# A two-layer graph network on one core: the first layer sorted in three parts of 72, 128 and 200 columns, GpSimd left with gathers alone, the norm split on ScalarE and VectorE, the relation weights made on TensorE

## The reference

```python
h = relu(layernorm(x))
neigh = segment_sum(h[src], dst, num_segments=3125)
x = x + relu(relu(((1 + eps) * h + neigh) @ W1 + b1) @ W2 + b2)

h = relu(layernorm(x))
weights = einsum('rb,bio->rio', coefficients, bases)      # 16 relations from 8 bases
msg[e] = h[dst[e]] @ weights[type[e]]
x = x + (h @ w_self.T).at[src].add(msg)
```

## Time and profile before

| | |
|---|---|
| three runs | 1696.48 us median (1687.71 to 1698.53) |
| profiled execution: span, first to last instruction | 1680.4 us |
| the profiled execution's own time | not listed apart from the three runs, which lie 7.3 to 18.1 us above its span |
| TensorE matmuls busy | 933.3 us, 56%, 5317 instructions |
| TensorE weight loads busy (they overlap) | 656.0 us, 39%, 5318 |
| VectorE busy | 749.9 us, 45%, 2213 |
| ScalarE busy | 413.4 us, 25%, 977 |
| GpSimd busy | 911.3 us, 54%, 843 |
| transfers | 101.58 MB, 60 GB/s; 43955 of 73343 packets under 512 bytes |

### The profile page before, as it was taken

The page is one execution under the profiler, slowest core; times in us unless marked ns, Lnnn a source line. Parts: engine busy times, 40 slices in busy tenths (PEclk is TensorE's granted clock), DMA queues, the critical chain, the costliest instruction groups (busy, mean ns, idle before and its releaser), DMA issues.

```text
span 1680.4 us, 22781 instructions
## 1 busy us (share of the span) xinstructions
PE 933.3 (56%) x5317; PEld 656.0 (39%) x5318; DVE 749.9 (45%) x2213; ACT 413.4 (25%) x977; POOL 911.3 (54%) x843
## 2 busy tenths in 40 slices
PE   1355275666238676766678997145354345453535
PEld 0223153444114344443356444134353344343535
DVE  8888463665934444593457543012121122121213
ACT  4662263552014333443345431000000000000000
POOL 4354655555866566765560003746656656566562
PEclk9955586777657777876789998567676567665667
DMA  3010222224122222212221685211111111111113
GB/s 73 0 57 20 73 52 61 54 55 57 47 67 60 54 56 59 59 41 60 57 57 10 196 285 152 54 35 43 44 40 45 45 36 47 40 43 44 39 46 55
DMA packets 73343, 101.58 MB, mean 60 GB/s; under 512 B 43955, under 2 KB 52836, under 8 KB 73036
## 3 DMA queue, kind: packets, MB, share of 16 engines
q0 software_dynamic: 33120, 67.88, 16.3%
q1 hardware_dynamic: 40166, 33.09, 7.2%
HBM read 70.88 MB, written 29.60 MB: 60 GB/s over the span
## 4 chain that ended last, share of the span: by engine, by line
PE 44%; issue 28%; DVE 12%; another core or an unknown queue 12%; ACT 1%; DVEq 1%; DMA 1%; POOL 1%; ACTq 0%; SPq 0%; POOLq 0%
PE ps L802 16%; PE ps L819 15%; PE ps L824 9%; PE ps L893 4%; DVE spare L554 1%; DVE chunk_hot L616 1%; ACT place_val_b L443 1%; DVE spare L587 1%; DVE node_hot L668 1%; DVE chunk_f L590 1%; DVE place_val_a L619 1%; DVE w_rel L679 1%; DVE spare L678 1%; POOL gathered L411 1%
## 5 line engine op out<-in xcount | busy, mean ns | idle before, releaser
L411 POOL DMA_INDIRECT gathered<-h_table,row_stage x420 | 469.9, 1119 | 309.8 <-issue 247.4
L411 POOL DMA_INDIRECT gathered<-z_table,row_stage x405 | 385.5, 952 | 385.8 <-issue 229.0
L819 PE MATMUL ps<-gathered,node_hot 128*125 128x128 f32 x1620 | 289.6, 326 | 350.1 <-issue 328.5
L443 ACT ACTIVATE place_val_b<-place_hot,code_b 125x128 f16<-125x128 f16 x800 | 343.8, 522 | 523.1 <-DVE place_hot L612 361.2
L819 PEld LDWEIGHTS ps<-gathered,node_hot 128*125 128x125 f32 x1620 | 258.4, 235 | 381.4 <-issue 381.1
L668 DVE TENSOR_SCALAR node_hot<-iota_f,key_of 128x250 f32<-128x250 f32 x405 | 130.6, 364 | 512.5 <-remote 368.6
L802 PE MATMUL ps<-chunk_hot,place_val_a 125*128 125x405 f16 (+2 forms) x800 | 280.0, 364 | 117.1 <-DVE place_val_a L619 58.6
L802 PE MATMUL ps<-chunk_hot,place_val_b 125*128 125x387 f16 (+3 forms) x1200 | 274.5, 292 | 50.0 <-issue 41.2
L824 PE MATMUL ps<-node_hot,gathered 128*128 128x250 bf16 x1260 | 193.6, 299 | 156.8 <-issue 117.6
L616 DVE TENSOR_SCALAR chunk_hot<-iota_h,chunk_f 125x405 f16<-125x405 f16 (+2 forms) x800 | 210.2, 341 | 13.1 <-issue 12.6
L824 PEld LDWEIGHTS ps<-node_hot,gathered 128*128 128x128 bf16 x1260 | 127.6, 106 | 211.1 <-issue 188.0
(11 more groups left out here) (128 smaller groups left out, 319.1 us busy)
## 6 DMA issues: line engine op xcount, KB each, us to landing
z_table<-spare SPq DMA_DIRECT2D x50, 448.0 KB
gathered<-h_table,row_stage POOLq DMA_INDIRECT x420
gathered<-z_table,row_stage POOLq DMA_INDIRECT x405
z_table<-spare SPq DMA_DIRECT2D x50, 52.0 KB
h_table<-gathered SPq DMA_DIRECT2D x1, 2100.0 KB
x_sb<-in_x SPq DMA_DIRECT2D x1, 1400.0 KB
out<-x_sb SPq DMA_DIRECT2D x6, 224.0 KB
row_stage<-row_of SPq DMA_DIRECT2D x81, 2.5 KB
```

The source lines that it names most:

```text
L411: pool.indirect_dma_start(place.rearrange("p j d -> p (j d)") if s < 2 else place, None, table, bass.IndirectOffsetOnAxis(ap=row_stage[s][ ...
L443: nc.scalar.activation(place_val_b[:, buf, i, :], place_hot[:, buf, :, i], ACT.Copy, scale=code_b[l][:, bass.ds(batch * BATCH + (c0 + i), ...
L819: last = T.matmul(psf[0:NP, bass.ds(offs[i] + half * D, D)], node_hot_of[s][:, k % HOTS[s], half * NP:(half + 1) * NP], gathered_of[s][:, ...
```

## The change

Layer one is sorted in three parts of 72, 128 and 200 columns, so there are four sorts. The first two use buckets of four tiles (7 buckets): their zero-one matrices and matmuls have 506 columns. The parts have 78, 132, 208 and 405 chunks, the rings hold 39, 44, 52 and 45. `BESIDE_ROUNDS` is now the whole number of rounds of the part ahead in each case but the last layer's own. The first sort has batches of its own (`sort_first`) without ScalarE: the code is multiplied into the chunk comparison. A code is now one number split in two halves, and each column takes two matmuls in every part.

GpSimd issues gathers and nothing else, written out one by one, straight from `row_of`; SyncE stages nothing. The norm's scaling and the first two parts of h are ScalarE's, the differences VectorE's, in two halves of 13 and 12 tiles. The relation weights are four matmuls of a block matrix of coefficients with the bases at the start, copied out by ScalarE, and turned to their layout through a table in memory. Layer two's sort is now decoded before the sums of layer one are copied out.

```diff
-SORTS = [(0, 0, 144, 3, 13), (0, 144, 256, 4, 11), (1, 0, 400, 5, 9)]
+SORTS = [(0, 0, 72, 4, 3, 13), (0, 72, 128, 4, 4, 11), (0, 200, 200, 2, 4, 13), (1, 0, 400, 2, 5, 9)]
+BUCKETS = [-(-TILES // tiles) for tiles in QUAD]
+WIDE = [2 * NP if tiles == 2 else 2 * NP + 2 * 128 for tiles in QUAD]
-HOTS = [13, 22, 9]
+HOTS = [13, 11, 26, 9]
-BESIDE_ROUNDS = [0, 3, 6]
-ALONE_ROUND = [0, 0, 3]
+BESIDE_ROUNDS = [0, 2, 3, 4]
+ALONE_ROUND = [0, 0, 0, 2]
...
         @block.sync
-            for p0, p1 in PARTS:
-                sp.dma_start(x_sb[p0:p1, :, :], x_rows[p0:p1, :, :]).then_inc(ld_x, 16)
+            for b in range(N_BASES):
+                sp.dma_start(bases_sb[b * IL:(b + 1) * IL, :, :],
+                             bases[b].rearrange("(ih il) o -> il ih o", il=IL)).then_inc(ld_b, 16)
-            stage_rows(sp, 0)
-            stage_rows(sp, 1)
+            for k, (t0_, t1_) in enumerate(HALVES):
+                sp.wait_ge(low_ready, k + 1)
+                for p0, p1 in PARTS:
+                    sp.dma_start(h_rows[p0:p1, t0_:t1_, :, :], h_parts[p0:p1, t0_:t1_, :, :]).then_inc(h_stored, 16)
+            sp.wait_ge(w_read, 4)
+            for m in range(2):
+                sp.dma_start(w_table.rearrange("(ih m il) (r o) -> m (il r) ih o", ih=IH, m=2, o=D)[m],
+                             w_turned[:, m * IH * D:(m + 1) * IH * D].rearrange("p (ih o) -> p ih o", o=D)).then_inc(w_stored, 16)
+            sp.wait_ge(w_stored, 32)
+            sp.dma_start(w_rel[:, :, :].rearrange("p r o -> p (r o)"), w_table).then_inc(wrel_ready, 16)
-            stage_rows(sp, 2)
...
         @block.gpsimd
-            pool.wait_ge(ld_c, 32)
-            add_bases(0, 3)
-            pool.tensor_tensor(h_sb[:, :, :], x_sb[:, :, :], neg_mean[:, :, :].to_broadcast([NP, TILES, D]),
-                               ALU.add).then_inc(centred, 1)
...
-            add_bases(3, BASES_FIRST)
-                with nc.gpsimd.Fori(0, ROUNDS[s]) as r:
-                    for g in range(GROUPS[s]):
-                        pool.wait_ge(staged[s][g], r * 16 + 16)
...
+            pool.wait_ge(h_stored, 64)
+            for s in range(NSORT):
+                pool.wait_ge(decoded, s + 1)
+                for k in range(CHUNKS[s]):
+                    slot = k % RING[s]
+                    if k % GROUP[s] == 0:
+                        if k >= RING[s]:
+                            pool.wait_ge(nhot_used, RING[0] + CHUNKS_BEFORE[s] + k + GROUP[s] - RING[s])
+                        elif s and k < RING[s - 1]:
+                            pool.wait_ge(nhot_used, RING[0] + CHUNKS_BEFORE[s] - RING[s - 1] + min(k + GROUP[s], RING[s - 1]))
+                    place = gathered_of[s][:, slot]
+                    pool.indirect_dma_start(
+                        place if s == LAST else place.rearrange("p j d -> p (j d)"), None, z_table if s == LAST else h_table,
+                        bass.IndirectOffsetOnAxis(ap=row_of[s][:, k:k + 1], axis=0)).then_inc(got[s][slot // GROUP[s]], 16)
...
         @block.scalar
+            for k, (t0_, t1_) in enumerate(HALVES):
+                for p0, p1 in PARTS:
+                    nc.scalar.dma_start(x_sb[p0:p1, t0_:t1_, :], x_rows[p0:p1, t0_:t1_, :]).then_inc(ld_x[k], 16)
+            normalise(0)
+            high(0)
+            normalise(1)
+            middle(0)
+            high(1)
+            middle(1)
+            act.wait_ge(w_ps, 4)
+            for q in range(4):
+                nc.scalar.copy(w_turned[:, q * BANK:(q + 1) * BANK], ps[:, q, :]).then_inc(w_read, 1)
...
         @block.vector
+            def sort_first(batch):
+                dve.wait_ge(batch_used, batch + 1)
+                V.tensor_tensor(place_hot[:, buf, :, :], iota_run[0:EP, :, :], each(place_h[0], P), ALU.is_equal)
+                own(V.tensor_tensor(first_hot[:, 2, buf], iota_run[0:EP, 0:FIRST, :], each(chunk_h0, FIRST), ALU.is_equal))
+                V.tensor_tensor(first_hot[:, 0, buf], first_hot[:, 2, buf], each(code_a[0], FIRST), ALU.mult)
+                V.tensor_tensor(first_hot[:, 1, buf], first_hot[:, 2, buf], each(first_b, FIRST), ALU.mult).then_inc(batch_ready, 1)
...
-            for s in (1, 2):
+            for s in range(1, NSORT):
                 rank_place(s)
...
-                rounds_beside(nc.vector, s - 1, node_hots, sort_batch, add_bases if s == 2 else None)
-                if s < 2:
-                    read_sorted(s)
-                    decode_rows(s)
-                    decode_keys(s)
-                    rounds_rest(nc.vector, s - 1, node_hots)
-                    rank_count(s + 1)
+                rounds_beside(nc.vector, s - 1, node_hots, sort_batch)
+                read_sorted(s)
+                decode(s)
+                rounds_rest(nc.vector, s - 1, node_hots)
+                if s < LAST:
+                    rank_count(s + 1)
```

More of the change, by code:

```diff
@@ new lines, in rank_count @@
+                own(V.tensor_scalar(need_i, tot_ps[:, 0:nb], float(P - 1), None, ALU.add))
+                own(V.tensor_scalar(need_i, need_i, 7, None, ALU.logical_shift_right))
+                own(V.tensor_copy(need_f, need_i))
+                own(V.tensor_tensor_scan(upto, need_f, need_f, 0.0, ALU.add, ALU.bypass))
+                nq = -(-CHUNKS[s] // P)
+                for q in range(nq):
+                    own(V.tensor_scalar(le_scr, upto, pidx[:, q:q + 1], 0.0, ALU.is_le, ALU.add,
+                                        accum_out=bucket_of[:, q:q + 1]))
@@ L781, in rank_sums @@
             def rank_sums(l):
+                nb = BUCKETS[l]
                 pe.wait_ge(count_ready, l + 1)
-                T.matmul(pre_ps, before[0:EP, 0:EP], count[:, :], start=True, stop=True)
-                T.matmul(tot_ps, ones[0:EP, :], count[:, :], start=True, stop=True).then_inc(prefix_done, 1)
+                T.matmul(pre_ps[:, 0:nb], before[0:EP, 0:EP], count_all[:, 0:nb], start=True, stop=True)
+                T.matmul(tot_ps[:, 0:nb], ones[0:EP, :], count_all[:, 0:nb], start=True, stop=True).then_inc(prefix_done, 1)
                 pe.wait_ge(bucket_of_ready, l + 1)
@@ L816, in add_up @@
                     pe.wait_ge(nhot_ready, r * RING[s] + (CHUNKS_BEFORE[s] + k + 1))
-                    for half in range(2 if s == 2 else 0):
+                    for half in range(2 if s == LAST else 0):
                         last = T.matmul(psf[0:NP, bass.ds(offs[i] + half * D, D)],
@@ L821, in add_up @@
                                         start=False, stop=False, skip_group_check=True)
-                    for part in range(SPLITS if s < 2 else 0):
-                        last = T.matmul(psf[:, bass.ds(offs[i], WIDE)], gathered_of[s][:, k, part, :],
+                    for part in range(SPLITS if s < LAST else 0):
+                        last = T.matmul(psf[:, bass.ds(offs[i], WIDE[s])], gathered_of[s][:, k, part, :],
                                         node_hot_of[s][:, k % HOTS[s], :], start=False, stop=False, skip_group_check=True)
@@ L828, in _ @@
             rank_sums(0)
-            for b in range(8):
+            zero_bank(7)
+            for b in range(2):
+                sort_first(b)
+            pe.wait_ge(kron_ready, 1)
+            pe.wait_ge(ld_b, 16 * N_BASES)
+            for m in range(2):
+                for q in range(2):
+                    T.matmul(ps[:, 2 * m + q, :], kron[:, m * IH:(m + 1) * IH, :].rearrange("p l r -> p (l r)"),
+                             bases_sb[:, q * BT:(q + 1) * BT, :].rearrange("p h o -> p (h o)"), start=True, stop=True).then_inc(w_ps, 1)
+            for b in range(2, COLS[0] // BATCH):
+                sort_first(b)
+            pe.wait_ge(w_read, 4)
+            for b in range(7):
                 zero_bank(b)
-            batches_alone(nc.tensor, 0, sort_batch, 0, ALONE[0])
-            pe.wait_ge(decoded, 1)
-            pe.wait_ge(h_ready, 1)
+            pe.wait_ge(h0_ready, 2)
             pe.wait_ge(eps_ready, 1)
```

404 lines of the change are left out of this document (192 added, 212 removed).

## The result

The changed kernel takes 1556.38 us (median of 4 runs, 1552.01 to 1560.11) against 1694.97 for the kernel before in the same comparison (4 runs, 1687.71 to 1698.53): ratio **0.918**, 95% interval 0.916 to 0.921. Predicted were 1567 us and a range of 1495 to 1660. Its profiled run took 1555.58 us, 2.0 above its span of 1553.6. The time lies in the range, 11 us under the forecast.

The account below looks back on a forecast made before the run. GpSimd's gathers, 1.25 us each plus stalls, were taken to pace both layers. 59 + 730 + 35 + 113.6 + 590.7 + 23 = 1551.3 us of span, with 16.1 above it 1567 us; range 1495 to 1660.

Parts of the forecast that it names:

- the round trip: In each gather gap, 2.4 us go over SyncE; with GpSimd waiting for TensorE itself, a gap loses 1.9 us.
- Layer two: Its gather stage: 19 gaps shortened from 6.35 us by 1.9 each, 590.7 us for 627.3, -37.
- rival 1: Gaps are not the round trip's to shorten; an earlier GpSimd only ends TensorE's free run earlier: 84 us back, 1651 (22%).
- Start: Before the first gather: smaller first sort and less GpSimd work bring it to 59 us from 144.8, -86, between -70 and -95.
- Layer one: Its gather stage, 730 us for 741.4, -11: issue 522.5, 25 gaps 66, two part ends at 37 each, long gathers 67.
- Drain: End of layer one after its last gather: 28.3 + 3 for decoding + 4 for a ring of 52 = 35 us, +7.
- Wide matmuls at nothing: Twice as wide matmuls for 210 chunks of layer one cost nothing, covered by GpSimd's 1.25 us per gather and its gaps.
- Rivals 3 and 5: 3: TensorE bounds layer one's first two parts, 84 us, 1651 (15%). 5: wide comparisons hold gathers up, 63 us, 1630 (5%).
- Dense stage and tail: Dense work between the layers: 113.6 us, -2, with no staging before the first gather; tail unchanged at 23 us.
- The overhead of 16.1 us: Median time of before over its profiled span, 1696.48 against 1680.4, added to the forecast span to give the time.
- Rival 2: GpSimd's 823 written-out gathers run slower, at up to 0.70 us more each; half of them would give 1855 us (8%).
- Rival 4: SyncE's 199 small copies cause TensorE's crawl; without them the gaps go too, 137 us less, 1430 (7%).

Follow-up runs that it names:

- experiment 1: Changed kernel again, 1555.05 us, 0.919 of before; and the kernel before without index copies, GpSimd unlooped and waiting for TensorE itself, 1593.11 us, 0.942.
- experiment 2: Changed kernel with SyncE's 192 index copies put back and awaited by GpSimd: 1623.18 us, 0.960 of before with the crawl; 1333.97 us, 0.946 without.
- Experiment 3: Changed kernel with the 192 index copies back but nobody waiting for them, on a chip without the crawl: 1317.73 us, 0.935 of before.
- experiment 4: Changed kernel with each next part's sort done one round earlier: 1493.51 us, 0.890 of before with the crawl; 1335.31 us, 0.946 without.
- experiment 6: Changed kernel with layer one's third part also in blocks of four tiles, comparisons and matmuls twice as wide: 1562.76 us, 0.924 of before, with the crawl.
- the covered kernel: Changed kernel with each next part's sort one round earlier, leaving each part's last round to sums alone: 1493.51 us, 0.890 of before, with the crawl.
- Experiment 5: Changed kernel with layer two's sums turned, half the TensorE instructions per chunk: 1535.82 us, 0.917 of before with the crawl; 1324.16 us, 0.938 without.

## Why the prediction was right, and where its steps were off

The main mechanism, the round trip, was right. That the span came within 2.3 us is in part luck: in the order of the table the steps were off by +8, -22, +12, +4, -2 and +3 us, and most of it cancels.

*Layer two* (-37 predicted, -38.5 measured): right in size and in cause. Experiments 1 and 2 take the wait out and put it in, and the stretch follows, 588 and 611 us, so rival 1 falls as to its conclusion. Its shape was wrong: I kept 19 gaps and shortened each by 1.9 us; there are 36, nearly all of 2.3 us, one per 10 gathers. A gap gave up 4 us, 77 for 19 of them. Only 2.4 of the 4 are the round trip: TensorE also moves again sooner, in the gaps shown 2.1 us after the last gather ended where before it took 3.7, and with the copies put back (experiment 2) 3.6. The prediction kept the 3.7; why they shrink is not shown. The number of gaps gave half of the 77 back: TensorE's free run is shorter when GpSimd returns sooner, 34 matmuls now; behind the gap of the earlier trace rows it went on for 64:

```profile
1132.48 9.55 PE L819 MATMUL ps<-gathered,node_hot 128*125 128x128 f32 x64 [0.33 <-DVE node_hot L668]
```

That is rival 1's premise, and the two sizes I took, 19 gaps and 1.9 us, were wrong in opposite directions.

*Start* (59 predicted, 66.8 measured, within its bound of -70). The sort began at 26.5 us for 22. From there to the decoding it took 29.6 us where the prediction had 29.3: a batch takes 2.32 us for 2.7, the wait for TensorE's bases 4.86 for 5, and VectorE's differences for the split of h stand between the batches. (The 1.6 us given as a batch's lower bound do not come out of the earlier trace rows: half the columns at full clock are about 0.06 us a matmul and not 0.1.) The step that was off is the end of the table. Its first half was sent at 54.55, but VectorE's last difference ended at 59.59, the second half was sent at 59.62 and landed at 66.5, 6.9 us later for the 4 of the prediction:

```profile
40.48 0.69 DVE L609 TENSOR_TENSOR place_hot<-iota_run,place_h 125x1024 f16<-125x1024 f16 x1 [4.86 <-PE ps L792]
...
57.83 1.76 DVE L666 TENSOR_TENSOR gathered<-spare,gathered 125x1536 bf16<-125x1536 f32 x1 [0.52 <-ACT gathered L418]
```

```profile
59.62 0.75 SPq L324 DMA_DIRECT2D h_table<-gathered  x2
```

*Layer one* (730 predicted, 707.6 measured). The part ends came near 182 and 410 us, ended on VectorE's decoding, and cost 24.2 and 30.7 for 37 each: 19 of the 22 us. I took the drain of before for their price. Experiment 3 shows that without the crawl one is 2.8 us. The other stalls came as predicted in sum and not in number, which is luck: 41 gaps over 0.6 us, 77.5 - 41 x 0.3 = 65 us, for 66 in 25 gaps. Long gathers: 461.2 - 418 x 0.949 = 64.5 us for 67.

*Drain* (35 predicted, 46.8 measured) is the step that was mis-sized most. The sort of layer two stands beside every round of the part ahead, as before, but its batches go into four rounds and not six: 12 in the last 52 chunks, where it was 8 in the last 44. In the drain itself ScalarE makes 80 of its copies, ten batches, for 40 in before. I added 4 us for the larger ring and nothing for the batches. With one free round it is 17.2 us (experiment 4).

*Wide matmuls at nothing*: near right for the stage, where experiment 6 has 12 us more of idle time and 21 less of gathers for 208 chunks, and 17 us where a drain is uncovered. Rivals 3 and 5, with 84 and 63 us, fall with it. *Dense stage and tail* came out 4.4 and 2.6 us above. The dense stage follows its granted clock: 118.0 us at 0.94, 116.6 at 0.97 in experiment 1, 115.1 at 0.99 in the covered kernel, 115.6 at 1.00 in before.

*The overhead of 16.1 us* was no overhead. In every run since, of either kernel, the time is about 2 us above the span; by that the profiled execution of before took some 1682 us, an estimate, and was quicker than each of the four runs. The forecast of the span was 2.3 us off; the 11 us by which the time was missed are this term.

*Rival 2*: gathers in straight code start 0.30 us after one another, as in the loop; false. Nor did straight code gain anything. The page "Runtime: NRT & Kernel Launch" of the Trainium skill (Instruction fetch mechanics) says that a taken branch stalls when its target lies outside the fetched window; whether the loop of before left that window no run here shows. *Rival 4*: the changed kernel has no copies and its TensorE crawls at 0.70 us all the same; false. What the crawl itself is stays open: it begins some 7 us after GpSimd resumes, ends 2 to 4 us after it stops, and is there on three chips and absent on two. Experiment 5 leaves open whether it counts instructions, time or bytes.

## To carry to other kernels

When an engine waits in a loop of two others, let it wait for the one that frees the buffer, and hand it the data in place; here taking the detour out was worth 97 of 135 us, and putting it back into the changed kernel cost 70. Keep one round without extra work at the end of each part, so that the next part's preparation is ready before the last buffers are full; it is worth 3% where TensorE is behind and costs 1% where it is not. Take a part's end price from the engine that is behind there, not from another drain. Compare two kernels by a third that ran on the same chip: two traces of the same layer two, on two chips with the crawl, differ by 7 us.

## What the runs showed of the hardware

- The kernel before takes 1411 us on two chips and 1678 to 1695 us on others. The changed kernel's gathers show where: in layer two no gap in 405 gathers (509 us, experiment 3) on the former, and 36 gaps (589 us) on the latter, where TensorE's loads and matmuls start on steps of 0.70 us until the gathers stop. In layer two of before, 215 of the 251 distances over 0.5 us between two matmuls are within 0.05 us of a whole multiple of 0.705. The change gains 8.1% where TensorE crawls; where it does not, the changed kernel with idle copies gains 6.5%.
- A gather that starts 0.17 to 0.19 us before VectorE enters a row of eight tensor_scalar comparisons of 405 columns (1.96 us together, 0.25 each) can be held until the row ends, 2.27 us instead of 0.95: 13 times in the changed kernel, 12 in experiment 3. Most gathers beside such rows are not held. The page "SBUF — State Buffer" of the Trainium skill (Who interferes with whom) says that tensor_scalar can take the port pair shared with GpSimd, and that the other side is blocked for the whole instruction; the held gathers agree with a block, but theirs lasts over eight instructions and not over one.
